# A two-pair-ahead convolution kernel: a bank-wise last half, fewer waits ahead of the second convolution, and one sum moved on VectorE

## What is computed

```python
def _gn(v, G=32, eps=1e-05):          # with 32 channels: each channel of each image by itself
    m = mean(v, axis=(H, W)); s = var(v, axis=(H, W))
    return (v - m) / sqrt(s + eps)

def conv_layer(X, W, beta, v, bias):
    B = sign(W[None] - mean(W) + us * std(W))          # 5 sign filters, us = -1, -0.5, 0, 0.5, 1
    alpha = solve(Bf.T @ Bf, Bf.T @ wf)                 # least squares
    W_eff = einsum('m,mhwio->hwio', alpha, B)
    for n in range(3):
        An = sign(clip(X + v[n], 0, 1) - 0.5)
        out += beta[n] * (conv3x3_same(An, W_eff) + sum(alpha) * bias[n])

x = x + conv_layer(_gn(x), ...)
```

## Time and profile before

| what | value |
|---|---|
| median of 3 runs | 198.26 us |
| the profiled execution's own time | 197.91 us |
| its span, first to last instruction | 195.0 us |
| PE busy | 174.5 us (89%) |
| DVE busy | 162.1 us (83%) |
| ACT busy | 153.9 us (79%) |
| POOL busy | 58.1 us (30%) |
| mean granted TensorE clock | 0.965 |

### The profile page before, as it was taken

How to read it: one execution, slowest core, us unless ns; L and a number is a source line. 1 busy time by engine, 2 the same in 40 slices (tenths; PEclk the granted TensorE clock), 3 DMA queues, 4 the chain that set the end, 5 groups by cost and what they waited for, 6 DMA issues and landing times.

```text
span 195.0 us, 4830 instructions
## 1 busy us (share of the span) xinstructions
PE 174.5 (89%) x1840; PEld 135.2 (69%) x1840; DVE 162.1 (83%) x406; ACT 153.9 (79%) x220; POOL 58.1 (30%) x74
## 2 busy tenths in 40 slices
PE   1897499399999999989999999999999999999960
PEld 1686486287777777767777777877787867768660
DVE  4579976979789999999899999899989999884332
ACT  2719949999789898989898989998989896953210
POOL 6264010506060505060515151424141424161000
PEclk9999669879999999999999999999999999999996
DMA  5999991054496989899978989889873838687525
GB/s 148 241 238 236 250 225 26 0 126 144 125 252 183 246 267 239 246 226 303 252 229 231 278 226 278 235 257 241 269 221 115 222 118 233 175 231 185 171 71 165
DMA packets 20349, 39.60 MB, mean 203 GB/s; under 512 B 9063, under 2 KB 9063, under 8 KB 20327
## 3 DMA queue, kind: packets, MB, share of 16 engines
q1 hardware_dynamic: 20016, 39.27, 74.2%
q10 hardware_dynamic: 310, 0.04, 0.1%
HBM read 13.15 MB, written 12.85 MB: 133 GB/s over the span
## 4 chain that ended last, share of the span: by engine, by line
PE 63%; DVE 15%; DMA 10%; ACT 7%; SPq 2%; issue 2%; DVEq 0%
PE conv_ps L805 34%; PE y_ps L827 11%; DMA s_odd<-s_even 9%; PE x_ps L755 6%; DVE raw_stats L597 4%; DVE y_nat L588 4%; ACT signs L359 4%; PE conv_ps L813 3%; DVE s_even L650 2%; PE conv_ps L808 2%; PE conv_ps L893 2%; PE conv_ps L775 2%; SPq L219 2%; ACT x_ch L354 1%; ACT filt L390 1%
## 5 line engine op out<-in xcount | busy, mean ns | idle before, releaser
L805 PE MATMUL conv_ps<-s_even,w_mm 128*64 128x448 f16 (+1 forms) x576 | 104.6, 336 | 1.6 <-DMA s_odd<-s_even 1.4
L808 PE MATMUL conv_ps<-s_odd,w_mm 128*64 128x448 f16 (+2 forms) x576 | 104.6, 324 | 0.0
L359 ACT ACTIVATE signs<-x_ch,neg_thr 128x784 f16<-128x784 f32 x96 | 85.4, 939 | 0.5
L805 PEld LDWEIGHTS conv_ps<-s_even,w_mm 128*64 128x64 f16 x576 | 61.1, 111 | 30.7 <-issue 6.2
L808 PEld LDWEIGHTS conv_ps<-s_odd,w_mm 128*64 128x64 f16 x576 | 61.1, 111 | 0.0
L322 POOL TENSOR_SCALAR lo_part<-signs,ratio_lo 128x1568 f16<-128x1568 f16 x15 | 23.6, 1572 | 99.5 <-DVE half_hi L643 92.5
L588 DVE SCALAR_TENSOR_TENSOR y_nat<-y_ps,y_const,x_nat 112x1024 f32<-112x1024 f32 (+1 forms) x32 | 36.8, 1149 | 11.7 <-PE y_ps L827 11.3
L372 ACT ACTIVATE y_ch<-conv_ps,y_scale 128x896 f32<-128x896 f32 (+1 forms) x32 | 29.1, 908 | 19.8 <-PE conv_ps L813 12.5
L827 PE MATMUL y_ps<-ident,y_ch 128*112 128x128 f32 x224 | 30.9, 278 | 1.5 <-DVE y_nat L588 1.5
L597 DVE BATCH_NORM_STATS2 raw_stats<-x_ch 128x6 f32<-128x448 f32 (+1 forms) x64 | 31.6, 555 | 0.8 <-ACT x_ch L354 0.8
L755 PE MATMUL x_ps<-ident,x_nat 112*128 112x112 f32 x192 | 25.4, 275 | 4.9 <-ACT x_ch L354 3.1
(11 more groups left out here) (119 smaller groups left out, 121.9 us busy)
## 6 DMA issues: line engine op xcount, KB each, us to landing
x_nat<-in_x SPq DMA_DIRECT2D x16, 448.0 KB, 5.8
out<-y_nat SPq DMA_DIRECT2D x16, 448.0 KB, 5.0
s_odd<-s_even SPq DMA_DIRECT2D x32, 203.0 KB, 3.3
s_odd<-s_even SPq DMA_DIRECT2D x32, 188.5 KB, 3.6
x_nat<-in_x SPq DMA_DIRECT2D x16, 336.0 KB, 4.8
out<-y_nat SPq DMA_DIRECT2D x16, 322.0 KB, 2.9
s_odd<-s_even SPq DMA_DIRECT2D x16, 29.0 KB, 3.1
x_nat<-in_x SPq DMA_DIRECT2D x16, 14.0 KB, 6.0
```

Source lines behind the costliest of these rows:

```text
L359: act.activation(signs[q % 2][:, n, :, a, :], x_ch[q % CH_SLOTS][:, :, a, :], ACT.Sign, bias=neg_thr[q % 2][:, n, a:a + 1]).then_inc(signe ...
L805: last = nc.tensor.matmul(low[:, 0:n * ROWS], wt, s_even[b][:, part, r0:r0 + 2 * n, t:t + H], start=first, stop=end)
L808: last = nc.tensor.matmul(high[:, 0:m * ROWS], wt, s_odd[b][:, part, r0:r0 + 2 * m, t:t + H], start=first, stop=end and not at_edge)
```

## The change

Five edits:

- PE: `bring_in(4, 0)` waits for the seventh `copy_in` instead of the eighth; the ten warm-up matmuls ahead of `convolve(1, 0)` go; four more are put ahead of `bring_in(2, 1)`.
- ACT: `sign(1, 2)` now stands ahead of `copy_in(3, 0)`.
- DVE: in round -1, `sum_high(1)` now stands ahead of pair 3's statistics.
- the end: `convolve(15, 1)` does bank 1 first, then `bring_out(15, 0)` into `x_ps`, then bank 0. Each bank is scaled, transposed and added by itself, on semaphores of its own.
- SP: the last half is stored as bank 1 (352 columns and the 32 wrapped ones) and then bank 0 (384 columns).

```diff
+LAST = PAIRS - 1
+LAST_BANKS = (1, 0)
 # sync
-                if real(p):
+                if real(p) and p != LAST:
                     store(p, 1)
+            sp.wait_ge(last_added, 1)
+            sp.dma_start(out_pairs[LAST][:, 45 * C:], y[:, 44 * C:55 * C]).then_inc(stored, 16)
+            sp.dma_start(out_pairs[LAST][:, 0:C], y[:, 55 * C:]).then_inc(stored, 16)
+            sp.wait_ge(last_added, 2)
+            sp.dma_start(out_pairs[LAST][:, 33 * C:45 * C], y[:, 32 * C:44 * C]).then_inc(stored, 16)
 # scalar
+            def scale_last(k):
+                j = LAST_BANKS[k]
+                n = half_bank(1)
+                act.wait_ge(last_conv, k + 1)
+                act.activation(y_ch[1][:, j * n:(j + 1) * n], conv_ps[1][:, j, 0:n], ACT.Copy, scale=y_scale[:])\
+                    .then_inc(last_scaled, 1)
...
-                if real(p):
+                if p == LAST:
+                    act.wait_ge(y_transposed, 2 * LAST)
+                    scale_last(0)
+                    scale_last(1)
+                elif real(p):
                     scale_out(p, 1)
...
             begin_signs(1)
+            sign(1, 2)
             copy_in(3, 0)
-            sign(1, 2)
 # vector
+            def add_last(k):
+                j = LAST_BANKS[k]
+                n = PER_BANK[1] * 128
+                at = OUT_COLS[1].start + j * n
+                dve.wait_ge(last_transposed, k + 1)
+                stt(y_nat[LAST % 2][:, at:at + n], y_ps[0:ROWS, j, 0:n], y_const[0:ROWS, :],
+                    x_nat[LAST % X_SLOTS][:, C + at:C + at + n], ALU.add, ALU.add).then_inc(last_added, 1)
...
                 if real(p):
-                    add_x(p, 0)
+                    add_x(p, 0, x_ps if p == LAST else y_ps)
                 if real(r):
                     add_root(divide_variance(r, invert_root(r)))
+                if p == -1:
+                    sum_high(q)
                 if real(t):
                     lane_moments(t, 0)
                     lane_moments(t, 1)
                     spread_lanes(t)
+                if real(q) and p != -1:
+                    sum_high(q)
                 if real(q):
-                    sum_high(q)
                     sum_low(q)
-                if real(p):
+                if p == LAST:
+                    add_last(0)
+                    add_last(1)
+                elif real(p):
                     add_x(p, 1)
 # tensor
                 if f == 0:
-                    if p == 1:
-                        warm_up(conv_ps[0], 10)
                     pe.wait_ge(hi_made, p + 1)
...
+            def bring_out_last(k):
+                j = LAST_BANKS[k]
+                pe.wait_ge(last_scaled, k + 1)
+                if k == 0:
+                    pe.wait_ge(y_added, 2 * LAST)
+                for i in range(PER_BANK[1]):
+                    at = j * PER_BANK[1] + i
+                    last = nc.tensor.transpose(y_ps[0:ROWS, j, i * 128:(i + 1) * 128],
+                                               y_ch[1][:, at * ROWS:(at + 1) * ROWS], ident[:])
+                last.then_inc(last_transposed, 1)
...
+                if p == LAST:
+                    convolve(p, 1, LAST_BANKS[0:1], last_conv)
+                    pe.wait_ge(x_copied, 2 * PAIRS)
+                    bring_out(p, 0, x_ps)
+                    convolve(p, 1, LAST_BANKS[1:2], last_conv)
+                    bring_out_last(0)
+                    bring_out_last(1)
+                    return
...
                 if real(t + 1):
-                    bring_in(t + 1, 0)
+                    bring_in(t + 1, 0, x_ps, 7 if p == -1 else None)
...
             pe.wait_ge(x_copied, 3)
             warm_up()
+            warm_up()
             bring_in(2, 1, y_ps, 4)
```

More of the change, by code:

```diff
@@ L141, in preact_conv_kernel @@
         y_added = sem("y_added")
+        last_conv = sem("last_conv")
+        last_scaled = sem("last_scaled")
+        last_transposed = sem("last_transposed")
+        last_added = sem("last_added")
         y_stored = [sem(f"y_stored{i}") for i in range(2)]
@@ L775, in warm_up, with convolve @@
                     nc.tensor.matmul(ps[:, 1, 0:128], ones[:], ones[:], start=True, stop=True)
-            def convolve(p, f):
+            def convolve(p, f, banks=(0, 1), done=conv_done):
                 b = p % S_SLOTS
@@ L787, in convolve @@
                     pe.wait_ge(edge_ready, 2)
-                for j in range(2):
+                for j in banks:
                     n = PER_BANK[f]
@@ L815, in convolve, with bring_out @@
                                                         start=False, stop=end)
-                last.then_inc(conv_done, 1)
-            def bring_out(p, f):
+                last.then_inc(done, 1)
+            def bring_out_last(k):
[8 more added lines that the diff above has]
+                last.then_inc(last_transposed, 1)
+            def bring_out(p, f, ps=y_ps):
                 k = 2 * p + f
@@ L826, in bring_out @@
                     at = (j % PER_BANK[f]) * 128
-                    last = nc.tensor.transpose(y_ps[0:ROWS, j // PER_BANK[f], at:at + 128],
+                    last = nc.tensor.transpose(ps[0:ROWS, j // PER_BANK[f], at:at + 128],
                                                y_ch[f][:, j * ROWS:(j + 1) * ROWS], ident[:])
```

8 lines of the change are left out of this document (5 added, 3 removed).

## The result

Twenty runs of the changed kernel gave a median of 195.05 us, twenty of the kernel before on the same chip 197.25 us; the ratio is 0.9857, 95% interval 0.982 to 0.9894. By the ratio that is 2.8 us (the medians differ by 2.2), where the forecast was 3.3 (194.9 us). Within 2% of before, as the forecast had it, though clearly faster. The time fits better than the gain does, and that is luck: the forecast started from 198.26 us, the median of three runs, and twenty runs put the kernel before at 197.25.

A forecast was written before the change was run, and what follows sets the result against it. PE and DVE were taken to bound the middle, running in step, and one chain the end. 197.91 - 1.4 (start) - 1.9 (end) = 194.6; with 0.35 to the median of the runs, 194.9 us, range 192.6 to 197.2.

The forecast's parts named there:

- Steps (1) and (2): At the start, pair 4's transposes begin at 34.8 instead of 37.20; pair 3's gathering waits until 41.4, PE keeps 1.05.
- Step (3): At the start, clock and low shift hold the second convolution until 44.4 to 44.8, leaving PE 1.75 us ahead.
- Step (4): DVE loses waits of 1.12 and 0.29, gaining 1.4 us; the middle keeps the smaller of 1.4 and PE's 1.75.
- rival C: In the middle, the shift becomes the bound and the kernel gets slower, 200.4 us at shifts of 5.3; chance 0.05.
- Step (5): Four extra warm-ups at the start count as 0; the first convolution can't start before its shift lands at 30.0.
- The end: The last pair, done bank by bank, ends at 193.1 instead of 195.0: 1.9 us gained, 0.9 to 2.2.
- (b): At the end, bank 0's matmuls finish 1.02 later, at 188.3; ACT scales 336 columns in 0.54, until 188.9.
- The signs: Expected in the trace: DVE's additions at 50.9 and 54.3 without wait, 1.4 kept at 164, last store at 188.8.
- A: The start gives nothing because the clock stays low for 6.8 us: 196.4 us; chance 0.14.
- D: At the end, three small hand-overs eat the gain, 0.9 us left: 195.9 us; chance 0.09.
- B: More than forecast: clock full at both places, DVE gets 2.1 and the end 2.2: 194.0 us; chance 0.12.

The follow-up runs named there:

- the start alone: The kernel before with only the edits at the start, without those of the end: 196.58 us, ratio 0.9952 to the kernel before.
- the kernel with the old sum: The changed kernel with the high sum of pair 1 back behind pair 3's statistics: 194.86 us, ratio 0.9864 to the kernel before.
- the two halves timed alone: The kernel before with only the start's edits (196.58 us, ratio 0.9952), and with only the end's edits (196.06 us, ratio 0.9918).
- no extra warm-ups: The changed kernel without the four extra warm-up matmuls: 196.07 us, ratio 0.9903 to the kernel before.
- shifts first: The changed kernel with SP issuing the shifts of pair p + 2 ahead of the store of pair p's first half: 195.94 us, ratio 0.992.
- the ten back: The changed kernel with the ten warm-up matmuls back ahead of the second convolution: 195.69 us, ratio 0.9921 to the kernel before.
- GpSimd behind: The changed kernel with GpSimd's low weighing of pair 1 waiting for the high sum of pair 1: 195.0 us, ratio 0.9895.
- all bulk behind: The changed kernel with the high sum in its old place and SP issuing shifts first, then loads, then both stores: 195.0 us, ratio 0.9912.

## Why the prediction was right, and where not

**Steps (1) and (2)** held. PE's transposes of pair 4 stand at 35.35 with 0.38 before them, and the pause before the gathering is 3.05, forecast 2.8. The copy's end was forecast at 41.4; it came at 42.0, and at 40.8 in the start alone; the difference is PE's low clock from 24 to 30 us.

**Step (3)** held in its place and failed in one term. It named the clock and the low shift as what holds PE back. By the record the clock fell in one of three ways: once at 24 for 6.8 us (the changed kernel's execution), once at 41 for 3.4 us as forecast (the kernel with the old sum), or never (the start alone, where only the warm-up's durations show a slow stretch). The low part was mis-sized: its sum "moves from 40.06 to about 40.3". It came at 41.68. Of the 1.62, 0.86 are the later moments (35.00 instead of 34.14; 33.76 in the start alone, so this is the clock's doing), 0.91 the high sum behind GpSimd, and 0.15 come back from `spread_stats`, which no longer waits. The price of the step was taken from the earlier trace rows, where nothing ran beside it; the moved instruction met GpSimd at its new place. The low shift landed at 43.19 + 3.08 = 46.27 instead of 45.6. The convolution had started at 44.17, ahead of the forecast 44.4 to 44.8, but stood until 46.40.

**Step (4)** held in its waits: 1.12 and 0.29 are gone. The forecast size was 1.4; the lead at the second pair was 0.9 in that execution, 2.2 to 2.3 in those without the low clock at 24. What failed is the sentence that the middle keeps the smaller of the two. By the thirteenth pair it had kept 0.3 of 0.9, 0.7 of 2.3 and 1.6 of 2.2, each read from one execution. The mechanism is that of rival C, at a smaller scale: with PE ahead, shifts that took 4.4 to 5.6 us stop it, in the changed kernel for 2.1 us beside the 0.9 at the second convolution, instead of 1.4 in all. I gave C only its extreme and put none of it into the forecast. Timed alone the start gave 0.95, with an interval from 0.1 to 1.8 us that holds the 1.4.

**Step (5)** was wrong where it said that the first convolution can't start earlier than at 30.1, because its shift lands at 30.0. It starts at 28.83 with the old place of the sum and at 29.43 in the start alone, and at 31.00 where the clock was low from 24 on. Where the slow stretch falls moves this start by over 2 us, and the forecast had no term for that. With it goes the lead: 0.9 in the changed kernel and 2.2 in the start alone, which have the same program up to the last pair.

**The end** held term by term: 0.54 for 336 columns as on the line through two rows; three transposes 0.54 (0.5); two additions of 384 columns in 1.32, 0.66 each (0.63); the last store at 190.44 (190.2), landed in 2.3. The span ended 1.8 earlier (1.9), timed 1.6. The eight transposes of half 0 ahead of bank 0 put the last scaling at 188.47, 1.15 behind the old 187.32, where (b) charged 1.0; splitting pays it back.

**The signs.** DVE's additions came at 51.41 and 54.80 with no wait, 0.5 later than forecast. But the 1.4 that should still be there at 164 was 0.3, and 0 at the last pair, so that the last store came at 190.44 and not at 188.8. Of the 3.3 this execution's span shows only the end's 1.8; its time of 194.96 is near the forecast because 1.1 us less lay outside the span than in the execution of before. That part of the agreement is luck. What supports the sum are the two halves timed alone.

**Rivals.** A is out by the run of the start alone, if narrowly (its interval ends at 0.9996), and D by the end's rows: 1.8 and not 0.9. B was partly true. Of the changed kernel's twenty runs, the seven with a recorded mean clock of 0.989 or more had spans of 190.8 to 192.6 us, the seven with 0.977 or less 191.7 to 195.2; the median of all twenty was not B's 194.0. C was true as a mechanism and not as the sign.

## What to carry to other kernels

An instruction moved to another place is priced by what runs beside it there: here VectorE's high sum and GpSimd's weighing waited for each other whole (0.97 became 1.88 us, 1.57 became 2.27), so look at GpSimd's row at the new time. A lead won at the start is kept only as far as the slowest transfer's slack allows; give part of the rival "the transfer becomes the bound" to the forecast itself. At the end of this kernel, splitting the last piece so that each small part flows through all engines paid more than reordering whole pieces (1.2 against 0.4 us). And compare more than one trace before you price a lead of under 1 us.

## What was not expected of the hardware

- VectorE and GpSimd in turns: 0.97 became 1.88, and 0.18 became 1.14 for 24 elements.
- The granted clock falls at different places in executions of the same start: 23.9 to 30.7 us in one, 41.4 to 44.8 in another, and by the record nowhere in a third; between the second additions of the first and the third lie 1.3 us. The pause of 3.05 us ahead of pair 3's gathering was followed by a fall in three of the kernels above (the old place of the sum, no extra warm-ups, shifts first) and by none in five (the changed kernel, the start alone, the ten back, GpSimd behind, all bulk behind).
- The recorded clock seems to miss slow stretches: it is 1.00 beside warm-ups of 0.24 us each in the start alone, against 0.13 in the changed kernel.
- Time outside the span is not constant: 2.9 us in the profiled execution of before, 1.8 in that of the changed kernel. A sum made against one execution's own time carries that 1.1.
